# Layer norm application moved from VectorE to ScalarE, with ScalarE's loop order rewritten, in a fused attention, FFN, RWKV and expert kernel

## The reference, cut to what matters

```python
def _layernorm(x, axis=-1, eps=1e-05):
    m = jnp.mean(x, axis=axis, keepdims=True)
    v = jnp.var(x, axis=axis, keepdims=True)
    return (x - m) / jnp.sqrt(v + eps)

x = x + _layernorm(attention(_layernorm(x)))
x = x + _layernorm(ffn(_layernorm(x)))
x = x + _layernorm(rwkv(_layernorm(x)))
x = x + _layernorm(experts(_layernorm(x)))
```

## Time and profile before

| | us |
|---|---|
| median of 3 runs | 2287.44 (2279.61 to 2292.96) |
| profiled execution | 2275.89 |
| its span | 2274.1 |
| busy: PE, DVE, ACT, POOL | 1811.0, 1594.9, 863.9, 701.7 |

### The profile page before, as it was taken

One profiled execution on the slowest core, in us unless ns is written; L12 is line 12 of the kernel. 1 busy time (PEld: TensorE's weight loads), 2 busy tenths in 40 slices (PEclk: granted clock), 3 DMA queues, 4 the chain that ended last, 5 costly groups with the idle time before them and its releaser, 6 DMA issues. The chain is left out here.

```text
span 2274.1 us, 32400 instructions
## 1 busy us (share of the span) xinstructions
PE 1811.0 (80%) x10526; PEld 1150.0 (51%) x10622; DVE 1594.9 (70%) x3315; ACT 863.9 (38%) x1838; POOL 701.7 (31%) x619
## 2 busy tenths in 40 slices
PE   0877998899789879978987997898766553399977
PEld 0444454455445445544544554555434342399963
DVE  3224589669758966976896697679669874477745
ACT  0253433345334333524342352434332121367732
POOL 0000043114103301420330142024017883466641
PEclk9788989899999999989999999989876676599989
DMA  4000000000000000000000000000012233676667
GB/s 137 0 1 10 0 2 1 20 0 1 10 11 1 1 20 1 1 10 11 1 1 20 1 1 10 11 1 1 10 38 98 102 110 116 223 236 204 195 211 272
DMA packets 83475, 119.48 MB, mean 53 GB/s; under 512 B 12697, under 2 KB 70109, under 8 KB 83168
## 3 DMA queue, kind: packets, MB, share of 16 engines
q1 hardware_dynamic: 69088, 80.29, 11.2%
q0 software_dynamic: 13056, 35.68, 4.2%
q10 hardware_dynamic: 1152, 1.18, 0.1%
HBM read 67.41 MB, written 51.79 MB: 52 GB/s over the span
## 5 line engine op out<-in xcount | busy, mean ns | idle before, releaser
L658 DVE TENSOR_TENSOR_SCAN s_buf<-r_work,kvb 128x512 f32<-128x512 f32 x256 | 353.6, 1383 | 0.0
L843 POOL TENSOR_TENSOR p_buf<-s_buf,r_work 128x512 f32<-128x512 f32 x128 | 152.9, 1194 | 460.1 <-DVE s_buf L658 452.8
L916 ACT ACTIVATE probs<-bank_s,nmx 128x256 f32<-128x256 f32 (+1 forms) x512 | 186.6, 450 | 109.8 <-DVE nmx L521 108.7
L843 POOL TENSOR_TENSOR r_work<-s_buf,r_work 128x512 f32<-128x512 f32 x128 | 158.1, 1237 | 189.2 <-DVE s_buf L658 188.9
L808 POOL TENSOR_TENSOR rstd<-vare,mhalf 128x4 f32<-128x4 f32 x48 | 48.4, 1008 | 506.8 <-DVE vare L454 506.7
L934 ACT ACTIVATE pt<-bank_s 128x1024 f32<-128x1024 f32 (+1 forms) x128 | 117.5, 918 | 208.5 <-PE bank_s L1224 208.5
L647 DVE TENSOR_TENSOR kvb<-r_work,bank 128x512 f32<-128x512 f32 x256 | 174.5, 682 | 20.5 <-PE bank L1342 12.7
L521 DVE TENSOR_REDUCE nmx<-bank_s 128x4 f32<-128x1024 f32 (+1 forms) x128 | 137.5, 1074 | 42.9 <-PE bank_s L1174 42.7
L1917 POOL DMA_INDIRECT y_rows<-w_in_ys,m_y_idx x144 | 141.8, 985 | 82.3 <-ACT w_in_ys L2005 43.9
L1341 PE MATMUL bank<-v_hi,sel_v 128*128 128x512 f32 x256 | 131.5, 514 | 14.8 <-DVE kvb L647 8.1
L1066 PE MATMUL bank_s<-wmask,ident_b 128*128 128x512 bf16 x340 | 103.9, 461 | 46.1 <-DVE vare L454 33.3
(11 more groups left out here) (403 smaller groups left out, 4170.2 us busy)
## 6 DMA issues: line engine op xcount, KB each, us to landing
m_xs<-x_rows SPq DMA_DIRECT2D x144, 144.0 KB
w_lo<-y_rows SPq DMA_DIRECT2D x4, 2048.0 KB, 21.7
w_hi<-y_rows SPq DMA_DIRECT2D x4, 2048.0 KB, 23.6
w_in_ys<-in_w SPq DMA_DIRECT2D x17, 256.0 KB, 4.0
x_new<-in_x SPq DMA_DIRECT2D x8, 512.0 KB, 3.8
x_after_rwkv<-x_b SPq DMA_DIRECT2D x8, 512.0 KB, 3.6
m_x_all<-x_after_rwkv SPq DMA_DIRECT2D x8, 512.0 KB, 4.1
out<-m_x_all SPq DMA_DIRECT2D x8, 512.0 KB, 3.5
```

What stands on the lines that cost most here:

```text
L658: V.tensor_tensor_scan(s_buf[:, n % 2, 1:S + 1], dec[:, n // HD, :], kvb[:, n % 2, :], 0.0, ALU.mult, ALU.add).then_inc(sem["state"], 1)
L843: G.tensor_tensor(p_slot(n), s_buf[:, n % 2, 0:S], rf[:, n // HD, :], ALU.mult).then_inc(sem["rs"], 1)
L916: ins = A(probs[:, n % 2, x, h * w:h * w + w], score_banks[n % 2][:, x, h * w:h * w + w], ACT.Exp, bias=nmx[:, n, 2 * x + h:2 * x + h + 1])
```

## The change

VectorE no longer applies the six norms. After the statistics and rstd it makes a bias, -mean * rstd, with one small instruction, and signals ScalarE, which applies each norm as four ACTIVATEs (Identity, scale = rstd, bias = that tile). VectorE waits for ScalarE before the three residual additions. ScalarE's order string becomes VectorE's. For steps in which ScalarE has instructions, its loop order is now: norm1 (norm), rnorm (copy x_b, norm), turn1, rturn, q, k, rproj0, rproj1, v, lat_scores, rproj3, lat_turn0, ..., mix, o_tok, resid1 (norm), norm2 (norm), turn2, ..., ffn_y, rresid (norm), resid2 (norm). So rnorm now stands ahead of turn1, and lat_scores ahead of rproj3. The order for the end is unchanged. A semaphore for the expert layer's loads is merged into another.

```diff
-    scalar="aarrrrrraarrarrraraaarrraraararrrrarrrrrararrraarraaraaraaarrrraaarraaaaaraararrarrarrrarrrraaaarraaaaaaarraa",
+    scalar="ararrrarrarrraararrrrraarraarararrarararraarrarararrarraarrararraarraraarrarararaarrrrarraararraaaaraaaaaraa",
...
                 ve.wait_ge(sem[rs], at(b, rs, n))
-
-            def normalize(side, dst, src, name):
-                for i in range(NT):
-                    ins = V.tensor_scalar(as_tiles(dst)[:, i, :], src(i), mv[:, side, i, 0:1], rstd[:, side, i:i + 1],
-                                          ALU.subtract, ALU.mult)
-                    if name:
-                        ins.then_inc(sem[name], 1)
-                return ins
+                V.scalar_tensor_tensor(nmean[:, side], mv[:, side, :, 0], -1.0, rstd[:, side], ALU.mult, ALU.mult
+                                       ).then_inc(sem[("mean", "r_mean")[side]], 1)
...
-                own.link(normalize(0, xn, lambda i: yt[:, i, :], None))
+                ve.wait_ge(sem["normed"], at(b, "normed", NT + 1))
                 if not (isinstance(b, int) and b == 0):
-                    ve.wait_ge(sem["x_kept"], at(b, "x_kept", 0))
+                    ve.wait_ge(sem["r_normed"], at(b - 1, "r_normed", NT))
...
-                own.link(normalize(1, r_xn, rtok, None))
+                ve.wait_ge(sem["r_normed"], at(b, "r_normed", NT + 1))
                 V.tensor_tensor(x_b[:], x_b[:], as_tiles(r_xn), ALU.add).then_inc(sem["x_final"], 1)
...
+            def normalize(b, side, n, dst, src, done=None):
+
+                mean = ("mean", "r_mean")[side]
+                sc.wait_ge(sem[mean], at(b, mean, n))
+                for i in range(NT):
+                    ins = A(as_tiles(dst)[:, i, :], src(i), ACT.Identity, bias=nmean[:, side, i:i + 1], scale=rstd[:, side, i:i + 1])
+                    if done:
+                        ins.then_inc(sem[done], 1)
+                return ins
+
             def attention_ffn(b):
+                normalize(b, 0, 1, xn, lambda i: x_new[:, i, :], "normed")
                 yield "norm1"
...
                 yield "ffn_tok"
+                normalize(b, 0, 4, xn, lambda i: (A0, A1)[i // 2][:, (i % 2) * D:(i % 2) * D + D]).then_inc(sem["normed"], 1)
                 yield "resid2"
...
-                A(x_b[:], x_tok[:], ACT.Copy).then_inc(sem["x_kept"], 1)
+                A(x_b[:], x_tok[:], ACT.Copy)
+                normalize(b, 1, 1, r_xn, lambda i: x_tok[:, i, :], "r_normed")
                 yield "rnorm"
...
+                    if name == "rresid":
+                        normalize(b, 1, 2, r_xn, lambda i: (R1, R2)[i // 2][:, (i % 2) * D:(i % 2) * D + D]).then_inc(sem["r_normed"], 1)
                     yield name
```

More of the change, by code:

```diff
@@ L53 @@
 PER = dict(
-    x_in=16, var=4, rstd=4, normed=2 * NT, turned=2 * NK, evened=2 * NK, x_free=1, a_final=1, own_a=30,
+    x_in=16, var=4, rstd=4, mean=4, normed=2 * NT + 2, turned=2 * NK, evened=2 * NK, x_free=1, a_final=1, own_a=28,
     pooled=1, q_ps=2, k_ps=2, v_ps=2, rq_ps=1, rkv_ps=1, q_sb=2, k_sb=4, v_sb=2, rq_sb=1, rk_sb=1,
@@ L60 @@
     f_lo=1, h_ps=NF, g_hi=NF, g_lo=NF, f_y=NF, fy_sb=2, fy_tok=1,
-    r_var=2, r_rstd=2, r_normed=NT, r_turned=NK, r_xt=NK, mix=8, proj=8, v_f=2, v_lo=1, k_f=2, dec=2, decay=1, r_f=2,
+    r_var=2, r_rstd=2, r_mean=2, r_normed=NT + 1, r_turned=NK, r_xt=NK, mix=8, proj=8, v_f=2, v_lo=1, k_f=2, dec=2, decay=1, r_f=2,
     rb=1, bonus_ps=1, bonus=1, v_bc=2 * HD, kv=2 * HD, state=2 * HD, rs=2 * HD, summed=8, o_sb=2, o_tok=1, o_diff=1, o_sq=1,
-    o_var=1, o_norm=1, o_back=1, o_aff=2, y_in=1, w_ps=1, x_final=1, x_out=16, own_b=3, own_c=18, x_kept=1,
+    o_var=1, o_norm=1, o_back=1, o_aff=2, y_in=1, w_ps=1, x_final=1, x_out=16, own_b=3, own_c=17,
 )
@@ L85 @@
     vector="ararrrarrarrraararrrrraarraarararrarararraarrarararrarraarrararraarraraarrarararaarrrrarraararraaaaraaraaaaaraa",
-    scalar="aarrrrrraarrarrraraaarrraraararrrrarrrrrararrraarraaraaraaarrrraaarraaaaaraarararrarrarrrarrrraaaarraaaaaaarraa",
+    scalar="ararrrarrarrraararrrrraarraarararrarararraarrarararrarraarrararraarraraarrarararaarrrrarraararraaaaraaraaaaaraa",
     gpsimd="arrrrrarrarrrarrrrrraraarrarararrrarrrarraararrarraaraaaaraaaraarrraaararraraaaaaarraaraaaarraarrrrarraraararaa",
@@ L172, in mid_token_layers @@
         act_own = ctx.enter_context(nc.semaphore("act_own"))
-        e_loaded = ctx.enter_context(nc.semaphore("e_loaded"))
         e_const = ctx.enter_context(nc.semaphore("e_const"))
@@ L222, in mid_token_layers @@
         rstd = sb("rstd", [P, 2, NT])
+        nmean = sb("nmean", [P, 2, NT])
         hiT = sb("hiT", [P, 2, S], F32R)
@@ L390, in _ @@
                 load_early_x(b)
[L391 to L396, removed]
+            sp.dma_start(e_ones, t["c_ones"]).then_inc(loaded, 16)
+            sp.dma_start(e_tri, t["c_wmask"][:, 0:P]).then_inc(loaded, 16)
+            sp.dma_start(e_gate_w, t["gate_w"].rearrange("(k p) n -> p k n", p=P)).then_inc(loaded, 16)
+            sp.dma_start(e_gate_b, t["gate_b"].partition_broadcast(P)).then_inc(loaded, 16)
+            sp.dma_start(e_w_raw[:, 0:W13], t["w13"][NE].rearrange("(k p) n -> p k n", p=P)).then_inc(loaded, 16)
+            sp.dma_start(e_w_raw[:, W13:], t["w2e"][NE]).then_inc(loaded, 16)
             for b in range(EARLY):
@@ L470, in attention_ffn @@
                 stats(b, own, 0, 1, lambda i: x_new[:, i, :])
-                normalize(0, xn, lambda i: x_new[:, i, :], "normed")
                 yield "norm1"
@@ L581, in attention_ffn @@
                 stats(b, own, 0, 3, lambda i: x_tok[:, i, :])
-                normalize(0, xn, lambda i: x_tok[:, i, :], "normed")
                 yield "norm2"
@@ L601, in attention_ffn @@
                 yield "ffn_tok"
-                own.link(normalize(0, xn, tok, None))
+                ve.wait_ge(sem["normed"], at(b, "normed", 2 * NT + 2))
                 V.tensor_tensor(x_tok[:], x_tok[:], as_tiles(xn), ALU.add).then_inc(sem["a_final"], 1)
@@ L611, in rwkv_head @@
                 stats(b, own, 1, 1, lambda i: x_tok[:, i, :])
-                normalize(1, r_xn, lambda i: x_tok[:, i, :], "r_normed")
                 yield "rnorm"
@@ L717, in expert_rows @@
                 own.start(B)
-                ve.wait_ge(e_loaded, 16 * 6)
+                ve.wait_ge(loaded, 16 * (n_load[0] + 6))
                 V.memset(e_biased[:, :, NE:], BIG)
@@ L945, in attention_ffn @@
                 yield "out"
+                normalize(b, 0, 2, xn, lambda i: as_tiles(y_tok)[:, i, :]).then_inc(sem["normed"], 1)
                 yield "resid1"
+                normalize(b, 0, 3, xn, lambda i: x_tok[:, i, :], "normed")
                 yield "norm2"
@@ L1022, in expert_rows @@
                     if b == 0:
-                        sc.wait_ge(e_loaded, 16 * 6)
+                        sc.wait_ge(loaded, 16 * (n_load[0] + 6))
                         A(e_w_hi, e_w_raw, ACT.Copy).then_inc(sem["q_sb"], 1)
@@ L1072, in turn @@
                         if k == 0:
-                            pe.wait_ge(sem[name], at(b, name, NT * n + i + 1))
+                            pe.wait_ge(sem[name], at(b, name, (NT + 1) * n + i + 1))
                         ins = T.transpose(dst[k][:, i * P:(i + 1) * P], as_tiles(src)[:, i, k * P:(k + 1) * P], ident[:])
```

## The result

The kernel after takes 2415.13 us in the median of four runs (2413.16 to 2419.67), against 2287.78 for the kernel before (2279.61 to 2292.96). The ratio is 1.056, with a 95% interval of 1.053 to 1.060. Its profiled execution took 2415.87 us, span 2414.1. That is 127 us slower, inside the range on record and 25 us beyond its number.

A forecast was written before the change was run, and what follows sets the result against it. Bound: VectorE in the middle, TensorE in the projections, a dependency chain around norms. Waits of 10.55 us an iteration, 73.9 for seven, plus 2.9 and 1.1: +78; clock 24.5: +102.5 on 2287.4, 2390 us; 8-in-10 range 2345 to 2425.

The forecast's parts named there:

- The price of a norm: Six norms moved to ScalarE: path grows by 0.89 us from SBUF and 0.25 from PSUM.
- The head: Start of the iteration: xT's copy waits behind x_b's copy and the second norm, delaying q matmuls, +3.7 us.
- The projections: Last projection waits for the decay's sigmoid, behind lat_scores' second exp and an exposed table load: +4.1; scan 3.4 us later.
- The seam: RWKV residual: norm behind two bias additions delays ffn_tok's statistics 2.1 us, added bias instruction 0.1; +2.2 in all.
- All waits: Sum of the delays at head, projections, RWKV residual and other norms: 10.55 us an iteration, 73.9 for seven.
- rivals 3 and 5: 3: swap free, only head and norms cost, 2354, 9%. 5: VectorE's work sets each iteration, so faster, 2229, 4%.
- two falls: TensorE's clock falls behind new idle times ahead of q and last projection: 1.75 us each, 24.5 in all, bounds 0 to 48.
- rival 2: Both delays, head and projections, but no lost TensorE clock: 2365 us, chance 22%.
- rival 4: Both clock falls long, 3.4 us each, plus an exposed softmax table load: +135, 2422 us, chance 11%.
- main case: Delays at head and projections plus some clock loss: 2390 us, own range 2372 to 2412, chance 52%.
- Outside the loop: Norms on the path of batch 0 cost 2.9 us, those at the end 1.1.
- The 11.6 us: Whole kernel: timed runs before lay 11.6 us above the profiled execution at their median, so the difference was added to 2378.

The follow-up runs named there:

- fillers in the two waits: Kernel after plus 16 throwaway TensorE matmuls in each new idle time, ahead of q and ahead of the last projection: 2360.1 us, ratio 1.033.
- the kernels with fillers: Throwaway matmuls in more TensorE idle times: kernel before 2283.4 us, ScalarE's order repaired at three places 2311.6, kernel after 2359.1.
- order only: Kernel before with only ScalarE's order string of the kernel after, all six norms staying on VectorE: 2327.0 us, ratio 1.016.
- rproj3 first: Kernel after with rproj3 put back ahead of lat_scores in ScalarE's order: 2337.4 us, ratio 1.022.
- rresid early: Kernel after with ScalarE's step rresid, the norm behind RWKV, moved ahead of ffn_y: 2379.8 us, ratio 1.040.
- the two repairs: Kernel after with turn1 back ahead of rnorm (alone 2379.1 us) and rproj3 ahead of lat_scores (alone 2337.4); both together 2323.7, ratio 1.015.
- its own copy with fillers: Kernel before with more throwaway matmuls in TensorE's idle times, nothing else changed: 2283.4 us, ratio 0.998 (0.996 to 1.000).
- all places repaired: Kernel after with turn1 ahead of rnorm, rproj3 ahead of lat_scores, rresid ahead of ffn_y, norms still on ScalarE: 2312.2 us, ratio 1.011.

## Why the prediction was right, and where its sizes were off

**The price of a norm.** 2.07 us for four tiles from SBUF and a bias instruction that releases ScalarE after 0.20: both as taken from the closing norm. From PSUM 1.93 and 1.94, estimated 1.95. With the clock held nearly equal in both kernels, norms alone cost 2.2 us an iteration; added up by stretches that the clock leaves alone it is 2.5 (0.9 at the head, 0.9 at norm2, 0.2 behind attention, 0.3 ahead of the statistics of the FFN's output and 0.2 behind them). The sum had 0.9 + 0.9 + 0.25 + 0.1 = 2.15.

**The head**: +3.60 measured, +3.7 predicted, by the route described, x_b's copy and the second norm ahead of xT's.

**The projections**: the wait is 4.17, predicted 4.1. To the first scan the delay grows by 5.55. Of this 5.87 - 3.70 = 2.2 is the slower projection, which leaves 3.4, as predicted. With fillers in the two waits, and so at full clock, the stretch from the copy of r_xT to the first scan takes 38.68 us instead of 35.37, +3.3. The prediction's own subtraction, 891.8 or 891.9 less 888.61, gives 3.2 to 3.3; it wrote 3.3 to 3.5 and took 3.4. The table load was exposed at 1.28 with the sigmoid directly behind it. The Trainium skill (ScalarE: Activation LUTs, "What ACT_TABLE_LOAD costs") has a drain of 1.38 with it; the trace shows 947.19 + 1.28 and the next ACTIVATE at 948.49, so no such time is added here. The new load for the softmax starts at 971.09 and ScalarE is idle 7.16 us before the ACTIVATE that needs it, so it cost nothing, as predicted.

**The seam**: +2.1, predicted 2.2, and moving the step removed 1.8 of it. The 0.3 that stay compare with the 0.1 (0 to 0.2) set down for the added bias instruction; the experiments do not show that it is this instruction.

**All waits**: 9.9 us an iteration with the clock nearly equal, and 10.3 added up by stretches (3.6 + 3.3 + 2.1 + 0.9 + 0.2 + 0.2), predicted 10.55. This part of the working held, and rivals 3 and 5 fell: the swap alone cost 1.6%, and VectorE's time was worth almost nothing.

**The clock was mis-sized.** The prediction took 1.75 us for each of two falls, 3.5 an iteration. Measured, it is 6.5 (16.8 us by which the iteration grew, less 10.3 of waits) to 6.9 (against the kernels with fillers). Where it lies shows in the stretches of an iteration, us, mean over all seven, each from the start of the instruction named before to the start of its own:

| up to | before | order only | after | rproj3 first | rresid early |
|---|---|---|---|---|---|
| copy of xT | 4.95 | 4.97 | 8.54 | 8.54 | 8.55 |
| copy of r_xT | 5.55 | 5.66 | 7.58 | 7.16 | 7.29 |
| first scan | 35.37 | 41.02 | 40.97 | 35.37 | 40.83 |
| remote | 12.65 | 12.47 | 13.55 | 11.39 | 12.70 |
| gate | 80.07 | 80.08 | 80.95 | 79.68 | 80.15 |
| addition behind attention's norm | 21.98 | 22.25 | 22.60 | 22.10 | 22.32 |
| copy of hiT | 6.21 | 6.21 | 7.10 | 7.10 | 7.10 |
| FFN output's statistics | 26.70 | 26.73 | 28.78 | 28.79 | 26.97 |
| last addition | 5.10 | 5.10 | 5.32 | 5.32 | 5.33 |

First, the two falls foreseen are longer than sized. The step took the lower of two values that its rows showed, and q and the projection lose 2.0 and 2.3 us (7.58 - 5.55, and 40.97 - 35.37 less the 3.3 of waits). Secondly, the step had no term for falls elsewhere. Between the first scan and the addition behind attention's norm 2.2 us more are lost (0.9 + 0.9 + 0.4), 0.9 of them in the middle, which the prediction had as long as before. No wait was found to which these belong. The late projection is not it: the kernel with only the order changed has it too, and takes there what the kernel before takes. These stretches differ from one iteration to the next in most of the kernels; in the kernel before the one from the first scan to remote takes 11.3 to 13.9 us, in the kernel after 13.5 or 13.6 every time. Over the loop the time at the lower level, from the rounded clocks, is about 2 x 1526 x 0.09 = 275 us against 2 x 1409 x 0.06 = 169. So rival 2 fell, and rival 4's sum (2422, with both falls long) was nearer than the main case's 2390, though not by its table load. The measured 2415 lies 3 us above the main case's own range (2372 to 2412), within the wider one. The Trainium skill (TensorE: Matmul & The Clock Gate, "What's actually happening") has idleness throttle and activity release the array; the fillers agree, as filling idle time behind equally late copies gave 55 us.

**Outside the loop** the prediction had 4 us, and the two profiles differ by 22 (8.5 ahead, 13.9 behind). The experiments show how much of that need not be the change's. Ahead of the loop, eight kernels whose code there is that of the kernel after took between 247.0 and 253.1 us, and the one with the code of the kernel before took 246.6 against 241.2. Behind it the seven of them whose code there is the same too took 625.6 to 638.1, and the two of the kernel before 624.2 and 628.0. Within those spreads a difference of 14 us cannot be put down to a cause from single profiles, and it stays open. The merged semaphore of the expert layer's loads, which lies there, was not tested by itself.

**Luck in the number.** Against the profiled execution the working gave 2378 us, and the profiled execution of the kernel after took 2415.87, 38 more: 19 in the loop, by the clock, and 18 outside it. The 11.6 us that the prediction added, because the timed runs before lay above the profiled one, bring the miss down to 25. The kernel after has no such distance (2415.87 profiled, 2415.13 in the median), so this term covered part of the error.

**Experiments that missed.** That rproj3 saved 78 us instead of 39 to 51, rresid 35 instead of 13, and the two fillers 55 instead of 31 to 40, is the same underestimate of the clock: take a wait away, and falls elsewhere that had no visible tie to it go too. By the table, rproj3 gains the 5.6 of its own stretch, and 3.9 between the first scan and the addition behind attention's norm; rresid gains 1.8 of its own and 1.9 there. Why they go is not settled. It is also the likely reason why the two repairs are not additive, which no run tested. No version tried is clearly faster than the kernel before; its own copy with fillers is the nearest, and its interval ends at no change.

## What to carry to other kernels

An engine that is busy 38% of the time can still be the wrong place for work: what counts is what stands behind the new instruction in its queue, and who waits for that. When work moves to another engine, write down that engine's order step by step, and treat each pair of steps that changes places as an edit with its own price; here two such pairs and one late step made 103 of 127 us, and the moved work itself 2.2 to 2.5 us an iteration. Price a new idle time of TensorE twice, once as the wait and once as the slower matmuls behind it.

## What the runs showed that was not expected

- The waits cost well over half as much again through the clock: 6.5 to 6.9 us an iteration on top of 9.9 to 10.3. A third of that lies in stretches to which hardly any wait was added (0.2 us).
- The same matmuls behind the same idle time of 0.74 us took 3.70 us in one iteration and 6.77 in another of the same execution, where the granted clock was 0.50 from 860 to 866 us. The kernel with all places repaired has iterations from 201.1 to 206.4 us.
- Equal code ahead of the loop took 241.2 and 246.6 us in two profiled executions, and equal code behind it up to 12.5 us more or less.
- Spending more on TensorE can save time: 15 of 16 extra matmuls in an idle time show in the trace as 3.6 us of work, and the kernel became 55 us shorter.
